# A graph network on one core: maximum pass and attention pass merged into one pass with a running maximum

## The chip, the core and the metric

The kernel runs on one NeuronCore of one Trainium2 chip. The time is that of one execution on the device in microseconds (us); lower is better. The engines have names here: PE is TensorE (its weight loads are PEld), DVE is VectorE, ACT is ScalarE, POOL is GpSimd, and SP is SyncE, which only issues DMAs in this kernel. DMA is a transfer between the chip's memories.

## The reference

12,500 nodes with 128 values each go through four layers, joined by 212,500 directed edges that are sorted by their end (`dst`) and go from `src` to `dst`. The change concerns the third layer, graph attention with 4 heads of 32 values. Its sums run over the edges of one `src` node (there the layer's `tgt` is `src`, and it gathers from `dst`):

```python
h = (node_features @ W + b).reshape(N, N_HEADS, F_HID)
s_i = jnp.einsum('nhf,hf->nh', h, a_i)
s_j = jnp.einsum('nhf,hf->nh', h, a_j)
eij = jax.nn.leaky_relu(s_i[tgt] + s_j[src], negative_slope=0.2)
m = jax.ops.segment_max(eij, tgt, num_segments=N)
ex = jnp.exp(eij - m[tgt])
denom = jax.ops.segment_sum(ex, tgt, num_segments=N)
alpha = ex / denom[tgt]
msg = alpha[:, :, None] * h[src]
out = jax.ops.segment_sum(msg, tgt, num_segments=N) + h
```

The other three layers (a relational convolution in two passes, a mean aggregation with batch norm, a plain mean aggregation) are not touched.

## The kernel before

The nodes lie in 98 blocks of 128. The edges are walked in steps: a step is up to 128 edges of one block, a group is K = 8 steps, and there are NG = 220 groups. Every edge pass runs the same way. POOL issues eight indirect DMAs for a group (`gather`, L1094), each of which brings 128 rows of `HROW` (128 values and 4 scores `s_j`, RW = 132 words) into a slot of the ring `G`, which has RING = 4 group slots. A one-hot matrix of 128 x 128 per step says which edge belongs to which node of its block, and PE multiplies with it.

The third layer has two edge passes.

`largest_pass` finds the largest `s_j` per node. Per group: POOL gathers the rows; SP stores them to `KEEP` in device memory (L1609); DVE splits the 32 scores per edge into three bf16 parts (`pieces`, L1735 to L1742, 5 instructions); PE turns them (5 transposes, L1655 and L1656) and ACT copies the result to `ROWS` (L1634). Then come four steps `pair(n)`: PE writes for two steps a matrix of 4 heads x 128 edges into two PSUM banks, where edges that are not of the node have a huge negative number (4 matmuls of 512 columns, L1665 and L1667, with the masks `MSEL` and `SEL` of the digits of the edge's place); DVE reduces them by maximum (`reduce`, L1750) and folds the result into `MJ` (`largest`, L1758, two per pair, each waiting for the one ahead). PE also runs 4 matmuls of 512 columns per group whose result nothing reads (L1677).

`attention_pass` then reads the groups back from `KEEP` (L1814), so POOL gathers nothing there. Per group: DVE builds the one-hots in bf16 (L1836), ACT casts them to f32 (`plain`, L1889), PE turns them (L1934) and ACT copies the turned ones (`turned`, L1897). PE looks up `s_i` and the maximum of every edge's node (`scores`, L1923, 8 matmuls in bf16), DVE makes the exponent (`exponents`, L1846 to L1855, 5 instructions), ACT takes exp (L1904), POOL multiplies the rows by it (L1876), PE clears three banks (`clear`, L1056) and sums with the one-hots (`main`, L1059, 8 f32 matmuls, which the trace shows as 16 records), and DVE adds the window of 9 blocks to `ACC` (`add_window`, L1066). Two windows of PSUM alternate.

On each engine the order is written by hand in `body(j, r)`, with offsets to groups further ahead. Block numbers come from tables in SBUF: `words_of` (L456) loads words into registers of the engine's queue, and behind it all instructions of that queue wait.

Of the kernel before, what the change touches and what calls it, by code (L numbers as in the profile page):

```python
# [9 lines left out]
P = 128  # L10
# [61 lines left out]
def build_gnn(nc, x, src, dst, etype, W1, loop1, b1, W2, loop2, b2, lw, lb, gamma, beta, gw, gb, attn, out):  # L72
# [5 lines left out]
    with ctx:  # L78
# [6 lines left out]
        POSA = sb("POSA", [P, SW])  # L85
# [39 lines left out]
        KEEP = dram("KEEP", [NG, P, K * RW])  # L125
# [338 lines left out]
        pool = [sem(f"work{i}") for i in range(20)]  # L464
# [1120 lines left out]
        READY = 35  # L1585
        MROW = 3 * K
        MBLOCKS = -(-NG * MROW // (2 * RW))

        def largest_pass(tag):
            fresh()  # L1590
            s_ids, s_pc, s_ts, s_sj, s_step, s_red, s_mx, s_c = (own(tag + n) for n in (
                "ids", "pc", "ts", "sj", "step", "red", "mx", "c"))
            s_got, s_st = [sem(tag + f"got{r}") for r in range(RING)], [own(tag + f"st{r}") for r in range(RING)]
            keep = KEEP.rearrange("g p w -> p g w")
            wtb, scrb = WT[:].bitcast(BF16), SCR[:].rearrange("p a c -> p (a c)").bitcast(BF16)
            SEL, MSEL = (wtb[:, i * K * P:(i + 1) * K * P].rearrange("p (k n) -> p k n", k=K) for i in range(2))
            ROWS = [scrb[:, i * 640:(i + 1) * 640] for i in range(2)]
            PLANES = [HT[:, i, :].bitcast(BF16)[:, HEADS * MROW:(HEADS + 1) * MROW] for i in range(2)]
            MPW = words.bitcast(BF16)[:, 0:NG * MROW]
            MP = MPW.rearrange("p (g m k) -> p g m k", m=3, k=K)  # L1600
            PIECES = [HT[:, i, :].bitcast(BF16)[:, 0:HEADS * 3 * K].rearrange("p (h q k) -> p h q k", h=HEADS, q=3) for i in range(2)]
            REST = SM[:, 1, :].rearrange("p (h k) -> p h k", h=HEADS)
            ROWST = PS[5].bitcast(BF16)[0:3 * K, 0:640]
            with nc.Block() as block:
                @block.sync
                def _(q):
                    def body(j, r, g):
                        q.wait_ge(s_got[r], 16 * K * (j + 1))
                        q.dma_start(keep[:, bass.ds(g, 1), :], G[:, r, :, :].rearrange("p k w -> p (k w)").unsqueeze(1)).then_inc(s_st[r], 16)  # L1609
                    groups(q, body)  # L1610
                    for s in s_st:
                        q.wait_ge(s, 16 * (NG // RING))
# [12 lines left out]
                def _(q):  # L1625
                    def ids(r, g):
# [513 lines left out]
```

## Time and profile before

| | |
|---|---|
| time, median of 3 runs | 13222.71 us (13216.57 to 13241.61) |
| the profiled execution's own time | 13216.57 us |
| its span in the trace | 13216.6 us |
| maximum pass, first piece to last reduction | 7817.3 to 10006.0 us |
| attention pass, first weights to end | 10021.2 to 10963.1 us |
| mean granted PE clock | 0.724 |

The profiled execution is one of the three timed ones, and its span is its time. Times inside the trace count from the span's start. A busy share says how long an engine worked, not that others waited for it; for that one needs the waits and the order in time.

### The profile page before, as it was taken

The page shows a single profiled execution, that of the slowest core. Times are in us where ns is not written, and L with a number is a line of the kernel's source. Part 1 is how long each engine was busy: PE and PEld are TensorE (multiplying, and loading weights), DVE is VectorE, ACT ScalarE, POOL GpSimd, SP SyncE. Part 2 cuts the span into 40 slices and gives each one's busy share as a digit, 9 for nine tenths or more (in the row PEclk, how much of TensorE's full clock was granted, in tenths as well). Part 3 has the DMA queues.
Part 4 walks back from the last instruction along what each step waited for, and adds up shares of the span by engine and source line. Part 5 has one row for each costly group of instructions (what it writes and reads, how often), then busy time and mean ns, then how long its engine had stood idle before and what let it go on. Part 6 is the DMA issues. An engine that isn't in the chain of part 4 may idle for free. (4 is left out here: it accounts for less than half of the span.)

```text
span 13216.6 us, 180443 instructions
## 1 busy us (share of the span) xinstructions
PE 7201.1 (54%) x38837; PEld 5498.7 (42%) x38948; DVE 7238.0 (55%) x15486; ACT 1724.0 (13%) x3850; POOL 8694.4 (66%) x9117
## 2 busy tenths in 40 slices
PE   7555655743333344444447956666668993333333
PEld 4444544433333344444446722222226772333333
DVE  5788888543333342222227976666667885333334
ACT  5000000200000022222220020000003552000000
POOL 0777777367777757777772137777775554777776
PEclk9777676866555566666668978888889996555665
DMA  5222222422222221111116823333333333222222
GB/s 189 63 52 52 52 52 52 152 73 53 53 53 53 53 56 53 53 53 53 53 53 168 202 85 108 108 108 108 108 109 116 126 126 83 54 54 54 54 54 66
DMA packets 704316, 1079.20 MB, mean 82 GB/s; under 512 B 174594, under 2 KB 483723, under 8 KB 704228
## 3 DMA queue, kind: packets, MB, share of 16 engines
q0 software_dynamic: 270832, 566.96, 16.8%
q1 hardware_dynamic: 301480, 449.08, 10.3%
q10 hardware_dynamic: 131916, 62.14, 1.8%
q8 instruction: 36, 0.59, 0.0%
q14 instruction: 52, 0.43, 0.0%
HBM read 717.19 MB, written 362.85 MB: 82 GB/s over the span
## 5 line engine op out<-in xcount | busy, mean ns | idle before, releaser
L1094 POOL DMA_INDIRECT G<-HROW,IDS x3424 | 3236.9, 945 | 1361.8 <-issue 1039.0
L1094 POOL DMA_INDIRECT G<-TAB,IDS x3328 | 3176.5, 954 | 1327.7 <-issue 996.6
L1194 PE MATMUL PSUM<-G,OH 128*128 x7040 | 1603.9, 420 | 2715.0 <-SPq L1126 2643.4
L1194 PEld LDWEIGHTS PSUM<-G,OH 128*128 128x128 f32 x7040 | 1491.9, 322 | 2827.0 <-issue 2827.0
L1433 POOL DMA_INDIRECT MSG<-G,IDS x1664 | 1617.0, 972 | 608.0 <-issue 506.5
L1421 PE MATMUL PSUM<-ACC,SCR 128*128 x3520 | 802.7, 417 | 974.9 <-ACT PSUM L1346 974.7
L1750 DVE TENSOR_REDUCE SM<-PSUM 128x8 f32<-128x1024 f32 x880 | 1077.2, 1224 | 398.4 <-PE PSUM L1667 301.1
L1177 DVE TENSOR_TENSOR ACC<-ACC,PSUM 128x129 f32 x1760 | 512.0, 291 | 1316.6 <-PE PSUM L1194 1090.6
L1177 DVE TENSOR_TENSOR X<-X,PSUM 128x128 f32 x1760 | 504.4, 287 | 1304.5 <-PE PSUM L1194 1076.0
L1421 PEld LDWEIGHTS PSUM<-ACC,SCR 128*128 128x128 f32 x3520 | 744.7, 317 | 1015.3 <-issue 1015.3
L1328 PE MATMUL PSUM<-G,OH 128*128 x3520 | 837.2, 414 | 588.0 <-DVE ACC L1090 390.3
L1394 DVE CAST SCR<-PSUM 128x1024 f32<-128x1024 bf16 x220 | 269.2, 1224 | 1541.9 <-PE PSUM L1410 1541.9
L1328 PEld LDWEIGHTS PSUM<-G,OH 128*128 128x128 f32 x3520 | 737.9, 310 | 626.5 <-issue 623.7
L1111 ACT COPY IDS<-IDXA 128x8 int32 (+1 forms) x624 | 122.3, 197 | 6087.4 <-PE PSUM L1194 4029.9
L1059 PE MATMUL PSUM<-G,OH 128*128 128x129 f32 (+1 forms) x7040 | 883.2, 279 | 29.2 <-DVE OH L1038 27.3
L1059 PEld LDWEIGHTS PSUM<-G,OH 128*128 128x128 f32 x7040 | 838.0, 191 | 112.4 <-issue 95.7
L1038 DVE TENSOR_TENSOR OH<-PSUM,DLOA 128x1024 f32<-128x1024 f32 x660 | 805.6, 1221 | 44.4 <-issue 42.8
L1876 POOL TENSOR_TENSOR G<-G 128x1024 f32<-128x1024 f32 x220 | 554.6, 2521 | 414.4 <-ACT G L1904 414.4
L1665 PE MATMUL PSUM<-SCR,WT 128*128 128x512 bf16 x1760 | 805.1, 457 | 36.8 <-DVE SM L1750 28.5
L1667 PE MATMUL PSUM<-SCR,WT 128*128 128x512 bf16 x1650 | 761.5, 462 | 0.0
L1066 DVE TENSOR_TENSOR ACC<-ACC,PSUM 128x1188 f32 x440 | 610.6, 1388 | 87.5 <-PE PSUM L1059 87.4
L1090 DVE TENSOR_TENSOR ACC<-ACC,PSUM 128x128 f32 x1760 | 500.2, 284 | 245.6 <-PE PSUM L1328 52.7
(348 smaller groups left out, 9577.3 us busy)
## 6 DMA issues: line engine op xcount, KB each, us to landing
KEEP<-G SPq DMA_DIRECT2D x220, 528.0 KB
G<-KEEP SPq DMA_DIRECT2D x220, 528.0 KB, 3.5
G<-MSG ACTq DMA_DIRECT2D x880, 66.0 KB, 2.2
G<-MSG SPq DMA_DIRECT2D x880, 66.0 KB, 2.1
G<-HROW,IDS POOLq DMA_INDIRECT x3424
G<-TAB,IDS POOLq DMA_INDIRECT x3328
TAB<-SCR SPq DMA_DIRECT2D x100, 512.0 KB, 2.6
TAB<-OH SPq DMA_DIRECT2D x96, 512.0 KB, 2.6
```

The lines of the kernel that those rows point to most:

```text
L1038: return q.tensor_tensor(OH[:, r % 2], bcast(iota.unsqueeze(1), P, K, P), bcast(dlo[:, bass.ds(g * K, K)].unsqueeze(2), P, K, P), op)
L1059: return q.matmul(window(n)[:, bass.ds(off, w)], hot, rows, start=False, stop=False, skip_group_check=True)
L1066: q.tensor_tensor(a, a, window(n).rearrange("p (a c) -> p a c", a=3)[:, :, 0:3 * RW], ALU.add).then_inc(s_add, 1)
L1094: q.indirect_dma_start(G[:, r, k, 0:row], None, table, bass.IndirectOffsetOnAxis(ap=IDS[:, r, k:k + 1], axis=0)).then_inc(s_got[r], 16)
L1177: q.tensor_tensor(a, a, sums(r, k), ALU.add).then_inc(s_add, 1)
L1194: m = q.matmul(sums(r, k), OH[:, r % 2, k, :], rows[k], start=True, stop=True)
L1328: m = q.matmul(slot(k)[:, 0:w], OH[:, r % 2, k, :], rows[k], start=True, stop=True)
L1421: m = q.matmul(PSUM[:, bass.ds(places[k], RW)], TURN[r % 2][:, k * P:(k + 1) * P], acc_of(regs[k], RW), start=False, stop=False, skip_grou ...
L1433: q.indirect_dma_start(MSG, bass.IndirectOffsetOnAxis(ap=IDS[:, r, k:k + 1], axis=0), G[:, r, k, :], None).then_inc(s_sc[r], 16)
L1665: q.matmul(bank.rearrange("p (h e) -> p h e", h=HEADS), MSEL[:, k, :], bcast(ROWS[r % 2][:, HEADS * P:(HEADS + 1) * P].unsqueeze(1), P, HE ...
L1667: m = q.matmul(bank, SEL[:, k, :], ROWS[r % 2][:, 0:HEADS * P], start=False, stop=True)
L1750: q.tensor_reduce(reduced(n), PSUM[:, (n % 2) * 1024:(n % 2 + 1) * 1024].rearrange("p (h e) -> p h e", e=P), AX.X, ALU.max).then_inc(s_red, 1)
```

## The change

`largest_pass`, `KEEP`, its stores and its reads are gone. One `attention_pass` gathers a group with POOL and keeps its rows in the ring `G` until they are summed. It holds a maximum per node that grows from group to group. After a group's maxima are folded in, `tops` writes the new exponent offsets of the 9 blocks of the group's window to `SI`, and keeps by how much the offset of the group's first block moved (`OLD`); ACT takes exp of that (`fade`), and DVE multiplies this block's sums in `ACC` by it (`rescale`). The one-hots no longer come from a comparison: PE multiplies the digit masks `MSEL` with `ROWS`, and ACT turns the result into 0 and 1 with a Relu with a bias (`plain`, `turned`). `scores` runs in f32 with 8 columns. The rows are weighted half by DVE (`weigh`, 4 steps) and half by ACT (`weights`, 16 instructions on 128 x 32). There is one window of sums (`SUMS`) where there were two. The 4 matmuls that nothing reads are gone. The order on each engine, with the group that each call works on relative to the body's group g:

- DVE: load of 8 block numbers; reduce 0 (g+1); rescale (g); exponents (g); reduce 1, largest 0 (g+1); weigh (g); reduce 2, largest 1 (g+1); pieces (g+2); reduce 3, largest 2 and 3 (g+1); tops (g+1); add (g)
- PE: scores (g); pair 1, 2, 3 (g+1); plain (g+1); rows (g+2); main (g); turned (g+1); pair 0 (g+2)
- ACT: ids (g+4); weights (g); plain (g+1); rows (g+2); turned (g+1); fade (g+1)
- POOL: the 8 gathers of one group after the other, each group after the ring slot's `main`

The diff, cut to its core:

```diff
-        KEEP = dram("KEEP", [NG, P, K * RW])
...
-        def largest_pass(tag):
...
+        def attention_pass(tag):
...
+            BANKS = [PSUM[:, i * 1024:(i + 1) * 1024] for i in range(2)]
+            SUMS = PSUM[:, 2048:3584]
+            ROWST = PS[7].bitcast(BF16)[0:3 * K, 0:640]
+            SCORES = PS[7][:, 320:320 + 2 * HEADS * K].rearrange("p (k h) -> p k h", k=K)
...
                 @block.gpsimd
...
                     def body(j, r, g):
                         q.wait_ge(s_ids, g + 1)
-                        wait(q, s_st[r], 16 * j)
-                        wait(q, s_pc, 5 * (g - RING + 1))
+                        wait(q, s_mm, g - RING + 1)
...
                         gather(q, r, HROW, RW, s_got)
...
+                    def weights(j, r, d):
...
+                        q.wait_ge(s_z, 4 * x + 4)
+                        q.activation(G[:, rx, :, D:RW], Z[rx % 2], ACT.Exp).then_inc(s_ex, 1)
+                        q.wait_ge(s_ex, x + 1)
+                        for k in range(K // 2, K):
+                            for h in range(HEADS):
+                                part_ = G[:, rx, k, h * HD:(h + 1) * HD]
+                                m = q.activation(part_, part_, ACT.Copy, scale=G[:, rx, k, D + h:D + h + 1])
+                        m.then_inc(s_wa, 1)
...
+                    def plain(j, r, d):
...
+                        q.wait_ge(s_hm, x + 1)
+                        wait(q, s_mm, x - 1)
+                        q.activation(OH[:, rx % 2].rearrange("p k n -> p (k n)"), BANKS[0], ACT.Relu, bias=ONES[:, 0:1], scale=1.0 / FAROFF).then_inc(s_of, 1)
...
+                    q.copy(ACC[:], bcast(ZERO[:, 0:RW].unsqueeze(1), P, NB, RW)).then_inc(s_clean, 1)
...
                 @block.tensor
...
+                    def scores(j, r, d):
...
+                        regs = blocks(q, BREGB, x)
+                        q.wait_ge(s_ot, x + 1)
+                        q.wait_ge(s_md, 4 * x + 4)
+                        wait(q, s_z, 4 * (x - 1) + 3)
+                        if there(x + 1):
+                            q.wait_ge(s_sj, x + 2)
+                        for k in range(K):
+                            m = q.matmul(SCORES[:, k, :], TURN[:, k, :], SIW[:, bass.ds(regs[k] * (2 * HEADS), 2 * HEADS)], start=True, stop=True)
...
+                    def plain(j, r, d):
...
+                        q.wait_ge(s_red, PAIRS * x + 3)
+                        for k in range(K):
+                            m = q.matmul(BANKS[0][:, k * P:(k + 1) * P], ROWS[rx % 2][:, HEADS * P:(HEADS + 1) * P], MSEL[:, k, :], start=True, stop=True)
...
+                    def main(j, r, d):
...
+                        places = words_of(q, REGS[96:97, :], x * 2 * K, K, 1536 - RW, first=K)
+                        wait(q, s_add, x)
...
                 @block.vector
...
+                    def weigh(j, r, d):
...
+                        q.wait_ge(s_ex, x + 1)
+                        rows = G[:, rx, own_part, 0:D].rearrange("p k (h f) -> p k h f", h=HEADS)
+                        q.tensor_tensor(rows, rows, bcast(G[:, rx, own_part, D:RW].unsqueeze(3), P, K // 2, HEADS, HD), ALU.mult).then_inc(s_wd, 1)
...
+                    def tops(j, r, d, first):
...
+                        [base] = words_of(q, GB, x, 1, NB - WIN, first=K)
+                        q.wait_ge(s_mx, (x + 1) * K)
...
+                        q.tensor_copy(OLD, was).then_inc(s_md, 1)
+                        q.tensor_tensor(TOPS, seen[:, :, 0:HEADS], MJW[:, bass.ds(base * HEADS, WIN * HEADS)].rearrange("p (b h) -> p b h", b=WIN),
+                                        ALU.add).then_inc(s_md, 1)
...
+                        q.scalar_tensor_tensor(seen[:, :, HEADS:2 * HEADS], TOPS, SLOPE, TOPS, ALU.mult, ALU.max).then_inc(s_md, 1)
...
+                        q.tensor_tensor(OLD, OLD, was, ALU.subtract).then_inc(s_md, 1)
...
+                    def rescale(j, r, d):
...
+                        [first] = words_of(q, BREGB, x * K, 1, NB - 1, first=K + 1)
+                        q.wait_ge(s_fe, x + 1)
+                        wait(q, s_add, x)
...
+                        q.tensor_tensor(rows, rows, bcast(FADE.unsqueeze(2), P, HEADS, HD), ALU.mult).then_inc(s_rs, 1)
+                        q.tensor_tensor(a[:, D:RW], a[:, D:RW], FADE, ALU.mult).then_inc(s_rs, 1)
...
+                        x, rx, jx = behind(j, r, 1)
+                        regs = blocks(q, BREGB, x) if there(x) else [None] * K
+                        reduce(j, r, 1, 0)
+                        rescale(j, r, 0)
+                        exponents(j, r, 0)
+                        reduce(j, r, 1, 1)
+                        largest(j, r, 1, 0, regs)
+                        weigh(j, r, 0)
+                        reduce(j, r, 1, 2)
+                        largest(j, r, 1, 1, regs)
+                        pieces(j, r, 2)
+                        reduce(j, r, 1, 3)
+                        largest(j, r, 1, 2, regs)
+                        largest(j, r, 1, 3, regs)
+                        tops(j, r, 1, regs[0])
+                        add(j, r, 0)
...
-        largest_pass("lp")
         attention_pass("at")
```

## Rows read from the trace of the kernel before

**Rows 1.** The page, part 1: busy time and share of the span of each engine.
```profile
PE 7201.1 (54%) x38837; PEld 5498.7 (42%) x38948; DVE 7238.0 (55%) x15486; ACT 1724.0 (13%) x3850; POOL 8694.4 (66%) x9117
```

**Rows 2.** Windows over the maximum pass and the attention pass: length, busy times, PE clock.
```profile
7817.30:10006.00 2188.70, 1387.06 (x5390) 543.70 (x5500) 1490.79 (x3737) 171.18 (x436) 1641.62 (x1741) 0.84 0.37 108
...
10021.20:10963.10 941.90, 860.47 (x7666) 739.55 (x7664) 802.68 (x1532) 480.43 (x657) 554.61 (x220) 1.00 0.38 124
```

**Rows 3.** Groups by line, maximum pass, 8200 to 9500 us: busy us, mean ns, idle before.
```profile
L1094 POOL DMA_INDIRECT G<-HROW,IDS x1042 | 983.1, 943 | 317.6 <-issue 317.6
L1750 DVE TENSOR_REDUCE SM<-PSUM 128x8 f32<-128x1024 f32 x520 | 636.6, 1224 | 234.8 <-PE PSUM L1667 180.8 <-issue 47.1
...
L1758 DVE TENSOR_TENSOR MJ<-MJ,SM 128x4 f32 x1041 | 166.5, 160 | 97.1 <-DVE MJ L1758 9.5
...
L1634 ACT COPY SCR<-PSUM 24x640 bf16<-24x640 bf16 x130 | 88.6, 681 | 1197.2 <-PE PSUM L1656 1197.2
```

**Rows 4.** Timeline, one group of the maximum pass: start us, us, instructions.
```profile
8409.73 1.06 DVE L1758 TENSOR_TENSOR MJ<-MJ,SM 128x4 f32 x4
...
8412.23 1.23 DVE L1750 TENSOR_REDUCE SM<-PSUM 128x8 f32<-128x1024 f32 x1 [1.43 <-issue]
...
8413.37 0.16 DVE L1735 COPY HT<-ACC 128x24 bf16 x1
...
8414.30 1.23 DVE L1750 TENSOR_REDUCE SM<-PSUM 128x8 f32<-128x1024 f32 x1
...
8414.36 0.60 PE L1655 MATMUL PSUM<-IDENTB,HT 128*24 128x128 bf16 x4 [3.45 <-DVE HT L1742]
...
8417.98 1.03 PE L1677 MATMUL PSUM<-USTB,LINB 128*128 128x512 bf16 x4
```

**Rows 5.** Line 456, maximum pass: the queue's load of 8 words, min/median/max ns.
```profile
L456 DVEq TENSOR_LOAD <-REGS x131: 594/597/612, 8200.2 to 9499.3; - x131
```

**Rows 6.** Windows inside one group of the maximum pass, columns as Rows 2.
```profile
8400.93:8404.35 3.42, 0.07 (x1) 0.07 (x2) 2.18 (x7) 0.00 (x0) 2.50 (x4) 0.93 0.34 89
8404.35:8407.76 3.41, 3.41 (x13) 1.44 (x14) 2.22 (x4) 0.78 (x2) 2.77 (x3) 0.57 0.56 188
```

**Rows 7.** Timeline, one group of the attention pass.
```profile
10406.54 0.61 PE L1934 MATMUL PSUM<-IDENTB,WT 128*128 128x128 bf16 x8
...
10406.98 0.67 PE L1056 MATMUL PSUM<-ZERO 128*128 128x396 bf16 x3
10407.09 0.19 DVE L1849 TENSOR_TENSOR SM<-SM,G 128x32 f32<-128x32 f32 x1
10407.18 1.01 ACT L1897 COPY SCR<-PSUM 128x1024 bf16<-128x1024 bf16 x1 [0.85 <-PE PSUM L1934]
...
10407.32 0.19 DVE L1851 SCALAR_TENSOR_TENSOR SM<-SM 128x32 f32<-128x32 f32 x1
10407.49 1.96 PE L1059 MATMUL PSUM<-G,OH 128*128 128x132 f32 x16
...
10409.59 1.39 DVE L1066 TENSOR_TENSOR ACC<-ACC,PSUM 128x1188 f32 x1 [0.39 <-PE PSUM L1059]
```

**Rows 8.** Line 456, attention pass: loads of 16 words and of 1 word.
```profile
L456 PEldq TENSOR_LOAD <-REGS x163: 1102/1104/1118, 10202.2 to 10896.4; - x163
L456 DVEq TENSOR_LOAD <-GB x163: 299/304/317, 10202.4 to 10896.7; - x163
```

**Rows 9.** Timeline, start of the maximum pass: gather beside DVE, DVE's clearing.
```profile
7802.53 1.99 DVE L1697 TENSOR_TENSOR ACC<-ACC 128x1760 f32<-128x1760 bf16 x1
7802.92 2.42 POOL L1094 DMA_INDIRECT G<-HROW,IDS  x1 [0.30 <-issue]
...
7808.76 8.64 DVE L1725 MEMSET ACC<- 128x10296 f32 x1 [2.21 <-issue]
```

**Rows 10.** Timeline, ACT: instructions with pointer operands, and the clearing of sums.
```profile
7773.27 1.65 ACT L658 ACTIVATE SCR<-X,NMR,RSTD 128x128 f32<-128x128 f32 x4
...
10008.39 2.39 ACT L1881 CAST ACC<-ZERO 128x2640 f32<-128x2640 bf16 x1 [13.42 <-PEq L475]
```

More of the change, by code:

```diff
@@ L461, in blocks @@
             return words_of(q, breg, g * K, K, NB - 1)
-        pool = [sem(f"work{i}") for i in range(20)]
+        pool = [sem(f"work{i}") for i in range(26)]
         assert [s.num for s in pool] == list(range(pool[0].num, pool[0].num + len(pool)))
@@ L1604, in largest_pass @@
-            with nc.Block() as block:
[L1605 to L1612, printed above, removed]
+            Z = [SM[:, 2 + i, :].rearrange("p (k h) -> p k h", k=K) for i in range(2)]
@@ L1614, in _, with behind, schedule, ring @@
+            def behind(j, r, d):
+                return j * RING + r + d, (r + d) % RING, j + (r + d) // RING
+            def schedule(q, early, body):
+                for i in range(-early, 0):
+                    body(0, i)
+                def ring(j):
+                    for r in range(RING):
+                        body(j, r)
+                rings(q, ring)
+            with nc.Block() as block:
                 @block.gpsimd
@@ L1640, in _, with ids @@
-                    for g in range(RING):
+                    def ids(x, rx):
+                        q.copy(IDS[:, rx, :], IDXB[:, bass.ds(x * K, K)]).then_inc(s_ids, 1)
+                    def weights(j, r, d):
+                        x, rx, jx = behind(j, r, d)
+                        if not there(x):
+                            return
+                        q.wait_ge(s_z, 4 * x + 4)
[6 more added lines that the diff above has]
+                        m.then_inc(s_wa, 1)
@@ new lines, in turned, with fade @@
+                    def turned(j, r, d):
+                        x, rx, jx = behind(j, r, d)
+                        if not there(x):
+                            return
+                        q.wait_ge(s_tm, x + 1)
+                        wait(q, s_sc, x)
+                        q.activation(TURN.rearrange("p k e -> p (k e)"), BANKS[1], ACT.Relu, bias=ONES[:, 0:1], scale=1.0 / FAROFF).then_inc(s_ot, 1)
+                    def fade(j, r, d):
+                        x, rx, jx = behind(j, r, d)
+                        if not there(x):
+                            return
+                        q.wait_ge(s_md, 4 * x + 4)
+                        wait(q, s_rs, 2 * x)
+                        q.activation(FADE, OLD, ACT.Exp).then_inc(s_fe, 1)
@@ L1641, in _, with body @@
+                    def body(j, r):
+                        x, rx, jx = behind(j, r, 4)
+                        if there(x):
+                            ids(x, rx)
+                        weights(j, r, 0)
+                        plain(j, r, 1)
+                        rows(j, r, 2)
+                        turned(j, r, 1)
+                        fade(j, r, 1)
+                    for g in range(2):
                         ids(g, g)
-                    rows(0, 0)
-                    ringed(q, body)
+                    q.wait_ge(s_c, READY)
@@ L1681, in _, with body @@
+                    def body(j, r):
+                        scores(j, r, 0)
+                        for n in range(1, PAIRS):
+                            pair(j, r, 1, n)
+                        plain(j, r, 1)
+                        rows(j, r, 2)
+                        main(j, r, 0)
+                        turned(j, r, 1)
+                        pair(j, r, 2, 0)
+                    schedule(q, 2, body)
                 @block.vector
@@ L1961, in build_gnn @@
+                    schedule(q, 2, body)
         tables_and_first("d0", load_relations(W1, loop1, b1))
```

364 lines of the change are left out of this document (136 added, 228 removed).

## The prediction

> **What bounds the kernel now.** I read the page first: no engine is busy for more than 66% of the span, so each pass has its own limit [rows 1]. Then the windows of the two passes that the change touches, then the lines, the timeline and the queue's loads of each.
>
> The maximum pass runs from 7817.3 to 10006.0, so 2188.7 / 220 = 9.95 us a group [rows 2]. The lines say why: a gather takes 943 ns and POOL's queue needs another 317.6 / 1042 = 305 ns before the next, so eight take 9.98 us, the whole group [rows 3]. POOL waits for nobody there; DVE (68% busy) and PE fit under it.
>
> The attention pass takes 941.9 / 220 = 4.28 us a group, with PE 91% busy at the full 2.4 GHz [rows 2]. There PE is the bound; DVE adds the window 0.39 us after PE let it [rows 7].
>
> Together a group costs 14.23 us, and both passes with the seam between them last from 7817.3 to 10963.1.
>
> **The change, part by part.** The 8 gathers stay, but POOL has only them: 9.98 us a group is the floor. Storing to and reading from `KEEP` goes, and is worth nothing by itself: neither pass waits for it. The seam goes too (15.2 us). Everything else of both passes now has to fit into one body, and the body's period T decides. So I add up DVE, from start to start, and then walk the waits.
>
> DVE, per group:
> - 4 reductions: one starts 1.14 us ahead of what follows it (8412.23 to 8413.37) [rows 4]: 4.56 us.
> - `largest`: four in a chain take 1.06 us, so 0.30 us each and 0.16 for the last [rows 4]. Pairs 0 and 1: 0.30 + 0.20 each, 1.00; pairs 2 and 3: three gaps, 0.90.
> - `pieces`: 8413.37 to 8414.30, 0.93 us [rows 4].
> - `exponents`: now 4 instructions on 128 x 32, one every 0.23 us [rows 7]: 0.92 us.
> - `rescale`: 128 and 4 columns. Not in the trace; between 0.16 for 4 columns [rows 3] and 0.19 for 32 [rows 7] for each, plus 0.1 for the wider: 0.40 us. Its load hides under reduction 0.
> - `weigh`: 512 columns, both inputs in SBUF. 1760 such columns take 1.99 us [rows 9] and 32 take 0.19 [rows 7], so 1.04 ns a column and 0.69 us; 0.61 from start to start. Bounds: 0.53 without any fixed part, and 1.55 if it has to wait for a whole gather (0.94 [rows 3]) each time; the small instructions with two SBUF inputs beside the gathers show no such wait (0.16 for 4 columns), so I stay low.
> - `tops`: nothing long lies ahead of it to hide its load of one word, 0.30 us [rows 8]. DVE's queue needed 1.43 us ahead of reduction 0 before, of which 0.60 is the load of 8 words [rows 4, 5]; the rest, 0.83, is unpacking, waits, addresses and a loop branch. For `tops` I take 0.30 + 0.60 of those, then four small instructions with computed addresses at 0.25: 1.66 us until its last starts.
> - `add`: again a bare load, 0.30 + 0.45 of queue steps, then 1.39 us [rows 7, 8], 1.30 from start to start; the load of 8 block numbers for the next body (0.60) hides under it, but for a branch every fourth time (0.1 on average): 2.15 us.
>
> Sum: 4.56 + 1.00 + 0.90 + 0.93 + 0.92 + 0.40 + 0.61 + 1.66 + 2.15 = 13.1 us. DVE alone would give T = 13.1, so what POOL and PE cost one after the other before (14.23) would be cheaper by 1.1 us a group.
>
> ACT, per group: ids 0.2, exp 0.25, 16 scalings, two Relus at 1.05, rows 0.68, fade 0.25. A scaling is not in the trace. Four instructions with two pointer operands on 128 columns take 1.65 us with 0.48 for the last alone, 0.39 apart [rows 10]; 96 columns fewer at 0.83 ns (0.68 and 1.01 us for 640 and 1024 columns bound that slope [rows 3, 7]) leaves 0.31. The floor is 0.19. I take 0.31: 5.0 us, 8.5 in all, under 13.1. Of one such instruction, the Trainium skill (ScalarE: Activation LUTs, What ACT_TABLE_LOAD costs) gives 186 ns + 0.83 ns a column + 93 ns for a pointer, with 93 ns of overlap. By that a scaling costs 0.21 us, and the sum of ACT falls to 6.9; T is the same by both.
>
> PE at full clock: `scores` and `main` are 16 records each, 1.96 us; 12 + 4 matmuls of 512 columns at 1.03 - 0.17 = 0.86 per pair, 3.4 us; plain and turned 0.5 each, rows 0.6, clears 0.5 [rows 4, 7]. That is 9.3 us of a body.
>
> **The walk.** Zero is the start of reduction 0. DVE: exponents (g) at 1.54, reduction 1 at 2.5, reduction 2 at 4.7, pieces (g+2) from 6.35 to 7.3, reduction 3 at 7.3, tops done at 11.1, add (g) at 11.7, next reduction 0 at 13.1. PE can turn the rows of g+2 only at 7.3. Behind them in its queue stands the load of 8 places for `main`: 1.10 us for 16 words [rows 8], 0.60 for 8 [rows 5]. After the transposes' dispatch (0.5) come load and unpacking (0.9), so clears start at 8.7 and `main` at 9.2, ending at 11.1. The scalings ended at 2.5 + 0.3 + 5.0 = 7.8 and are not late; `add` at 11.7 is not held either. Then `turned` on PE to 11.7, its Relu on ACT to 12.8, the waits and addresses of `scores` 0.2, `scores` to 15.0. DVE wants it at 13.1 + 1.54 = 14.6. It is 0.4 late: T = 13.5 at the full clock, and now the loop pieces, rows, main, turned, scores, exponents is the bound, with DVE just under it. The bound has moved to waits.
>
> The order in this loop is what makes the clock count. Before, PE sat idle for 3.45 us in each group [rows 4], and the stretch behind that was granted 0.57 of the clock, nearly all of it at the lower level of 1.2 GHz [rows 6]; it cost nothing, because POOL was the bound. In the new body PE has only pair 3 and plain (1.3 us) between the end of pair 2 (about 3.2) and the rows at 7.3, each after a reduction. The four idle matmuls that filled in before are gone. So I expect a like stretch at 1.2 GHz once a body, 3.4 us long as in rows 6, and just where rows, clears and `main` run, which are 2.9 us of the loop. At half speed such a stretch does 1.7 us of work less; the queue's load absorbs 0.3 of it. T = 13.5 + 1.4 = 14.9.
>
> **The sum.** Start: DVE's preparation ends at 7808.8, where it cleared part of `ACC` before [rows 9]; ACT clears all 12,936 columns instead. 2640 took 2.39 us [rows 10], so 11.7 us, and the first pieces start at about 7820 where they started at 7817.3. 220 bodies and two that run ahead with half their work are 221 T. The end is at 7820 + 221 x 14.9 = 11113, against 10963 before: +150 us. The profiled execution's time is 13216.6, all of it span, and becomes 13367; the median lies 6.1 higher: 13373, say 13370. In general the time is 10080 + 221 T, and no change lies at T = 14.22. A change within 0.2% (26 us) can hardly be told from none.
>
> **The rivals.**
> 1. DVE stays the bound, as PE's short gaps do not take the clock down. For it: pairs and plain break the idle time up, and PE works 9.3 of 13.5 us. Against it: in the maximum pass a nearly empty window was followed by one at 0.57 [rows 6], and here 1.3 us in 4.1 is not much more. T = 13.4 to 13.6, time 13060. It decides from T = 14.1 down. Chance 0.28.
> 2. Two stretches at half clock in a body, or one that never ends: rows, main, turned and scores are 6 us of work; another 1.8 us lost gives T = 16.7, time 13770. Against it: PE at half clock is busy for most of the body, which brought the clock back within one window before. Chance 0.10.
> 3. The gathers become the bound again. Beside instructions of DVE on 1760 columns a gather took 2.42 us, not 0.94 [rows 9]; beside `pieces` and `largest` they did not stretch [rows 3]. `weigh` meets one or two gathers a group, for 10.7 to 11.5 us in all, under T. It would need four at 2.4: 16 us, time 13616. Chance 0.03. By the Trainium skill (SBUF — State Buffer, Who interferes with whom), DVE and GpSimd share a port pair, an instruction of DVE with two SBUF inputs contends with GpSimd instructions that read SBUF, and the loser waits for the whole instruction. By that rule `weigh`, `rescale` and `tops` speak against this change, since either side may be the one that waits.
> 4. The ring starves: a gather may start only after `main` of four groups ago. It then has from 11.1 to 2T + 6.35 = 36, and needs 10 us and a few to land. Chance 0.02.
> 5. The change is only a trade: T lands within 0.12 of 14.22. Chance 0.08.
>
> **How the numbers follow.** The forecast, slower with T between 14.4 and 15.9 (13262 to 13594 by itself), has 0.49. With rivals 2 to 4 slower has 0.64, same 0.08, faster 0.28. The range has to hold rival 1 but for its fastest end, T = 13.4 (13040), and reaches to T = 16.4 (13700) above: 0.8 together.
>
> **What the profile after would show.** The stretch as one pass of about 3290 us; POOL idle before gathers, waiting for `main` of four groups ago; a DVE wait before exponents for `scores`, 0.4 us if the clock is full and 1.5 to 2 if not; PE's clock at 0.8 to 0.9 in the pass; ACT waiting for `turned`. The walk is wrong if DVE waits ahead of a reduction or of `pieces`; the sum is wrong if DVE's queue needs more than 0.9 us ahead of `tops` or `add`; the clock step is wrong if the pass shows 1.00 or under 0.7.

## The result, and the profile after

The changed kernel takes 13301.22 us (median of 4, 13288.21 to 13321.94) beside 13220.29 us for the kernel before (median of 4, 13216.57 to 13241.61). The ratio is 1.006, with a 95% interval of 1.0046 to 1.0074: slower by 0.6%, 81 us. Forecast were 13370, the range 13040 to 13700, and slower with a chance of 0.64. The profiled execution is the slowest of the four (13321.94 us, span 13320.1); the rest of this section is read from it.

Part 1 of the page, beside [rows 1]. No engine is near full; ACT has gained most, by the scalings.
```profile
PE 7349.2 (55%) x41367; PEld 5824.4 (44%) x41588; DVE 7216.4 (54%) x16580; ACT 2582.6 (19%) x7590; POOL 8163.6 (61%) x8897
```

The new pass as one window, first reduction to last `add`, columns as [rows 2]:
```profile
7835.50:11062.60 3227.10, 2398.69 (x15612) 1609.09 (x15829) 2284.55 (x6375) 1502.70 (x4836) 1648.81 (x1741) 0.89 0.16 37
```
The adds start from 7856.85 to 11062.59 in 219 steps, so the period between two adds is T = 14.64 us, where 14.9 was forecast and 14.22 would have been no change. DVE is busy for 71% of the pass, PE for 74%, POOL for 51%. Nobody is full: the pass is held by waits. The clock is 0.89.

The groups by line, 9000 to 10500 us (102 groups; columns as [rows 3]):
```profile
L1094 POOL DMA_INDIRECT G<-HROW,IDS x813 | 769.9, 947 | 727.8 <-PE PSUM L1781 390.6 <-issue 337.2
L1865 DVE TENSOR_REDUCE SM<-PSUM 128x8 f32<-128x1024 f32 x407 | 497.2, 1222 | 79.5 <-issue 68.6 <-PE PSUM L1736 9.2
...
L1781 PE MATMUL PSUM<-G,OH 128*128 128x132 f32 x1616 | 268.7, 336 | 0.0
...
L1943 DVE TENSOR_TENSOR ACC<-ACC,PSUM 128x1188 f32 x101 | 140.6, 1392 | 131.2 <-PE PSUM L1781 123.3 <-issue 7.9
...
L1901 DVE TENSOR_TENSOR G<-G 128x512 f32<-128x512 f32 x102 | 70.5, 691 | 0.0
...
L1887 DVE TENSOR_TENSOR SM<-PSUM,G 128x32 f32<-128x32 f32 x101 | 19.2, 190 | 40.2 <-PE PSUM L1717 40.2
```
A gather takes 947 ns beside `weigh`, as it did without it, and `weigh` never waits. POOL stands before gathers until `main` (L1781) has freed the ring. PE's transposes (L1765) wait for `pieces` in each group, 85.3 us in 102 times, and `scores` waits for the Relu behind `turned` 94 times (48.1 us): the loop of the prediction's walk is there. DVE waits in two places of each group: 123.3 / 101 = 1.22 us ahead of `add` for `main`, and 40.2 / 101 = 0.40 ahead of the exponents for `scores` (L1717). And there is a line that the prediction had nothing for: reductions (L1865) wait 68.6 us for "issue".

From the list of waits, same stretch: us in total, times, longest.
```profile
DVE ACC L1943 <- PE PSUM L1781: 123.3, 85, 2.5
...
PE PSUM L1765 <- DVE HT L1857: 85.3, 102, 1.1
...
DVE SM L1865 <- issue: 68.6, 24, 3.1
```
The last line is 24 waits of 2.86 us, not 400 small ones. The stretch holds 26 turns of the loop. The timeline shows which reduction it is, DVE alone:
```profile
9305.97 1.39 DVE L1943 TENSOR_TENSOR ACC<-ACC,PSUM 128x1188 f32 x1 [1.27 <-PE PSUM L1781]
9310.24 1.23 DVE L1865 TENSOR_REDUCE SM<-PSUM 128x8 f32<-128x1024 f32 x1 [2.88 <-issue]
...
9322.74 1.39 DVE L1943 TENSOR_TENSOR ACC<-ACC,PSUM 128x1188 f32 x1 [1.65 <-PE PSUM L1781]
...
9336.30 1.39 DVE L1943 TENSOR_TENSOR ACC<-ACC,PSUM 128x1188 f32 x1 [0.49 <-issue]
```
It is reduction 0, behind the fourth `add` of a ring, where DVE's queue jumps back to the start of its loop. The queue's own records of line 1070 (the loop's end), 9000 to 10500: times, shortest/median/longest ns, first and last start.
```profile
L1070 DVEq COMPARE_BRANCH  x26: 62/63/63, 9008.9 to 10487.0; - x26
...
L1070 DVEq FUSED_REGOPS  x26: 105/105/105, 9011.7 to 10489.8; - x26
```
The branch starts at 9008.9 and takes 0.06; the next instruction starts at 9011.7. Over all the turns of the pass the gap, from the end of the branch to the next instruction, has a median of 2.76 us. In the maximum pass of the kernel before it was 0.23. It shows in the periods between adds, by their place in the ring: 13.76, 13.98, 14.26 and 16.75 us (means from the 20th group on).

Five packets of the instruction queue go with each turn, and the page counts 314 of them, beside 52 for the kernel before:
```profile
q14 instruction: 314, 2.57, 0.1%
```

Now the clock, in windows over one slow body (the `add` of 9305.97 to that of 9322.74) and one fast (to 9336.30):
```profile
9313.60:9317.00 3.40, 2.92 (x12) 1.20 (x12) 2.89 (x11) 2.71 (x13) 2.02 (x3) 0.50 0.21 48
9317.00:9320.40 3.40, 2.41 (x12) 1.79 (x13) 2.33 (x9) 1.80 (x2) 0.00 (x0) 0.50 0.06 14
...
9327.20:9330.60 3.40, 1.81 (x9) 0.47 (x7) 3.21 (x6) 3.37 (x17) 2.63 (x3) 1.00 0.25 60
9330.60:9334.00 3.40, 1.83 (x19) 1.34 (x20) 2.71 (x11) 2.06 (x4) 1.89 (x2) 1.00 0.24 60
```
and PE in both bodies:
```profile
9318.69 1.17 PE L1776 MATMUL PSUM<-ZERO 128*128 128x396 bf16 x3 [0.48 <-issue]
9319.66 2.82 PE L1781 MATMUL PSUM<-G,OH 128*128 128x132 f32 x16
...
9333.17 0.67 PE L1776 MATMUL PSUM<-ZERO 128*128 128x396 bf16 x3 [0.75 <-issue]
9333.68 1.96 PE L1781 MATMUL PSUM<-G,OH 128*128 128x132 f32 x16
```
At 1.2 GHz clears and `main` are slow and `add` waits 1.65 us; at 2.4 GHz `main` takes 1.96 and `add` starts after 0.49 us of DVE's own queue. The fast body lasts 13.56 us. Of 1500 us, 370 were granted half the clock, 3.6 us a group. They are not spread evenly: by place in the ring a body has 1.2, 2.9, 2.6 and 7.3 us of it (means from the 20th group on), and the 7.3 are in the body with the jump, where PE waits for the late reduction 0 as well (0.90 us at 9311.52, and the pairs behind it are slow). So the jump and the clock are not independent of each other.

### The profile page after: what moved, and what is told of

It reads as the page before. It is cut to its first block and busy times, and to the rows that moved or that the text cites. A ratio compares the mean times of both kernels' runs of the same rounds, so it can differ in the third digit from the quotient of the medians.

```text
span 13320.1 us, 189431 instructions
## 1 busy us (share of the span) xinstructions
PE 7349.2 (55%) x41367; PEld 5824.4 (44%) x41588; DVE 7216.4 (54%) x16580; ACT 2582.6 (19%) x7590; POOL 8163.6 (61%) x8897
## 5 line engine op out<-in xcount | busy, mean ns | idle before, releaser
L1194 PEld LDWEIGHTS PSUM<-G,OH 128*128 128x128 f32 x7040 | 1496.0, 323 | 2828.2 <-issue 2828.2
L1865 DVE TENSOR_REDUCE SM<-PSUM 128x8 f32<-128x1024 f32 x880 | 1075.1, 1222 | 165.8 <-issue 135.4
L1328 PEld LDWEIGHTS PSUM<-G,OH 128*128 128x128 f32 x3520 | 739.3, 310 | 631.8 <-issue 629.1
L1734 PE MATMUL PSUM<-SCR,WT 128*128 128x512 bf16 x1760 | 715.9, 407 | 164.4 <-DVE SM L1865 150.6
L1651 ACT ACTIVATE G<-G 128x32 f32<-128x32 f32 x3520 | 771.8, 309 | 7.1
L1736 PE MATMUL PSUM<-SCR,WT 128*128 128x512 bf16 x1540 | 625.3, 406 | 0.0
L1781 PEld LDWEIGHTS PSUM<-G,OH 128*128 128x128 f32 x3520 | 578.1, 246 | 32.2 <-issue 24.8
L1781 PE MATMUL PSUM<-G,OH 128*128 128x132 f32 x3520 | 567.4, 329 | 4.2 <-ACT G L1651 4.2
L1717 PEld LDWEIGHTS PSUM<-SI,SCR 128*128 128x128 f32 x3520 | 410.4, 192 | 216.2 <-issue 216.2
```

Of the source, the lines that this page charges most:

```text
L1194: m = q.matmul(sums(r, k), OH[:, r % 2, k, :], rows[k], start=True, stop=True)
L1328: m = q.matmul(slot(k)[:, 0:w], OH[:, r % 2, k, :], rows[k], start=True, stop=True)
L1651: m = q.activation(part_, part_, ACT.Copy, scale=G[:, rx, k, D + h:D + h + 1])
L1734: q.matmul(bank.rearrange("p (h e) -> p h e", h=HEADS), MSEL[:, k, :], bcast(rows_[:, HEADS * P:(HEADS + 1) * P].unsqueeze(1), P, HEADS, P ...
L1736: m = q.matmul(bank, SEL[:, k, :], rows_[:, 0:HEADS * P], start=False, stop=True)
L1781: m = q.matmul(SUMS[:, bass.ds(places[k], RW)], OH[:, rx % 2, k, :], G[:, rx, k, :], start=False, stop=False, skip_group_check=True)
```

## The experiments

So there were two candidates for what a body costs above 13.5: the jump back of DVE's loop (theory A, that DVE waits for instructions) and PE's half clock (the clock step of the prediction, B). A third question was what the loads in the queues cost. All ratios are against the kernel before, on the same chip. The three sets of runs were on three chips, where the kernel before takes 13237.97, 13216.56 and 13220.16 us, so runs of different sets are compared by ratios and by T.

**Padding that was none.** Two kernels with empty instructions ahead of DVE's loop:
```
                     assert c.n == READY, c.n
+                    for _ in range(96):          # second kernel: 256
+                        q.nop(nofuse=True)
                     q.wait_ge(s_clean, 1)
```


> The changed kernel with 96 empty instructions on DVE just ahead of the loop of the new pass, run once; nothing else differs. Theory A (instruction fetch): DVE's loop of four bodies has 322 instructions and lies over the border of what its instruction store holds, so every jump back waits 2.75 us for instructions. 96 instructions further on it lies within two lines of 256. Then the gap after DVE's loop branch falls from 2.75 us to 0.2, the long fourth period (16.8 us) becomes like the other three (13.6 to 14.2), the packets of the instruction queue fall from 314 to under 100, and the time falls by up to 54 x 2.75 = 148 us, to 13150 to 13190: faster than the kernel before. Theory B (the fourth body is long because of what its instructions wait for, scores and a clock at half speed, and the jump back only shows it): the gap and the periods stay, 13300.

> As the run with 96, but with 256 empty instructions, one whole line of 256, so that the loop lies as it did against the lines. Theory A: nothing changes; the gap of 2.75 us stays, every fourth period is 16.8 us, 13300 (13290 to 13320). If empty instructions help in some other way than by where the loop lies, the time falls as with 96.

13294.02 us, ratio 1.004 (1.0026 to 1.0054), and 13296.04 us, 1.0044 (1.0027 to 1.0061); gaps of 2.73 us and 314 packets in both. But the compiled program is one instruction longer than that of the changed kernel in both cases, so these empty instructions moved nothing. The two runs test neither theory. They are worth keeping as repeats: T is 14.61 and 14.51, beside 14.64. Differences of T of 0.1 are no more than that spread. Of the figure in the first text: the Trainium skill (Runtime: NRT & Kernel Launch, Instruction fetch mechanics) says that the store is two lines of 256 instructions and that a jump to an instruction outside them waits for a fetch.

**The clock.**
```
+                    def busy(n):
+                        for _ in range(n):
+                            q.matmul(PSUM[:, 3468:3580], LINB[:], USTB[:, 0:112], start=True, stop=True, ...)
...
                         for n in range(1, PAIRS):
                             pair(j, r, 1, n)
+                            busy(12 if n > 1 ... else 0)
                         plain(j, r, 1)
+                        busy(12 ...)
```


> The changed kernel with 36 more matmuls a body on PE, whose result nobody reads (112 columns each, into columns of PSUM that nothing uses): 12 behind pair 2, 12 behind pair 3, 12 behind plain; DVE's code stays where it was. The clock step of my prediction: PE's idle time there brings a stretch at 1.2 GHz in each body, on the path rows, clears, main, turned, scores; with the clock at 2.4 GHz throughout, a body loses 0.7 us and more: 13301 - 221 x 0.7 = 13146, and 12990 if it was 1.4. Rival (DVE is the bound in three bodies of four, and the jump in the fourth): the clock goes up from 0.87 to 0.95 and more, the wait of exponents for scores goes, and the time falls by its 0.40 us a group at most, to 13210 to 13300.

13165.16 us, ratio 0.9945 (0.9928 to 0.9961), T = 13.92: now the kernel is faster than before the change. The gap at the jump is unchanged, 2.73. Groups by line, 9000 to 10500:
```profile
L1781 PE MATMUL PSUM<-G,OH 128*128 128x132 f32 x1712 | 210.1, 276 | 0.0
...
L1949 DVE TENSOR_TENSOR ACC<-ACC,PSUM 128x1188 f32 x107 | 149.0, 1392 | 55.1 <-PE PSUM L1781 41.7 <-issue 13.4
```
`main` costs 210.1 / 107 = 1.96 us a group where it cost 268.7 / 101 = 2.66, and the wait of `add` for it falls from 1.22 to 0.39. T fell by 0.72, about these 0.70. The half clock has become less and has moved: 218 us of 1500 are still at 1.2 GHz, no record of `main` is stretched any more, and what is stretched are a quarter of the pairs and a seventh of the added matmuls. The three short periods are 13.55, 13.19 and 13.51.

**The loads.** DVE's two loads of a window base and PE's load of eight places, moved ahead (with the 96 empty instructions, which do nothing):
```
+                        y = behind(j, r, 0)[0]
+                        top = words_of(q, GB, x, 1, NB - WIN, first=K)[0] if there(x) else None
+                        base = words_of(q, GB, y, 1, NB - WIN, first=K + 2)[0] if there(y) else None
                         reduce(j, r, 1, 3)
...
-                        tops(j, r, 1, regs[0])
-                        add(j, r, 0)
+                        tops(j, r, 1, regs[0], top)
+                        add(j, r, 0, base)
...
+                        places = places_at(j, r, 0)
                         rows(j, r, 2)
-                        main(j, r, 0)
+                        main(j, r, 0, places)
```


> The kernel with 96 empty instructions, and three loads of registers moved ahead of waits: DVE's window base for tops and for add ahead of reduction 3, PE's eight places for main ahead of the transposes. If DVE's queue ahead of tops and add is on the path (my sum had 0.30 us for each bare load), the time falls against the run with 96 by up to 221 x 0.6 = 130 us, to 13020 to 13060. If the loop rows, main, turned, scores, exponents is the bound and only PE's load counts, it falls by 221 x 0.3 = 65 us or less, and DVE waits longer for scores or for main. If DVE's queue had these loads done while the engine worked, nothing changes.

13122.85 us, ratio 0.991 (0.9893 to 0.9926), T = 13.72. It took off more than both loads of DVE together could (0.9 of T against 0.6), so PE's load counts too, and `main` is slow less often (303 ns a record for 336). The waits say more:
```profile
DVE SM L1871 <- issue: 174.3, 137, 3.2
...
DVE ACC L1947 <- PE PSUM L1784: 20.8, 31, 1.3
```
DVE's loads are hardly hidden in their new place: besides the jump, reduction 3 (L1871) now stands 0.84 us for issue in each body, where `tops` and `add` had 0.60 and 0.49. What has gone is the wait of `add` for `main`, 1.22 us a group before and 0.19 now. That points to PE's load as the source of the gain; but the three were moved together, and no run parts them.

**Where DVE's loop lies.** Real instructions instead of empty ones, in the time in which DVE waits for ACT's clearing:
```
                     assert c.n == READY, c.n
+                    spare_columns = SM[:].rearrange("p a c -> p (a c)")
+                    for i in range(119):         # others: 16, 55
+                        c.inc(q.memset(spare_columns[:, i:i + 1], 0.0))
+                    c.hold()
                     q.wait_ge(s_clean, 1)
```


> The empty instructions of the first two runs never reached the program: it grew by one instruction, DVE's loop stayed where it was, and so they tested nothing. Here 119 real ones stand in their place, each a memset of one column that nobody reads, during 13 us in which DVE waits for ACT's clearing anyway. In the compiled program DVE's loop of 322 instructions then begins at instruction 3423, not at 3304. Theory A (fetching instructions): where the loop lies decides whether the jump back waits. The gap after DVE's loop branch falls from 2.75 to about 0.2 us, every fourth period comes down from 16.7 us to 14.0, packets of the instruction queue fall from 314 to under 100, and the time falls by up to 54 x 2.75 = 148 us, to about 13150, faster than the kernel before. Theory B (the fourth body is long for other reasons): gap, periods and time stay. By the Trainium skill (Runtime: NRT & Kernel Launch, Instruction fetch mechanics) the store holds two lines of 256 instructions; in the changed kernel the loop touches three such lines if they are counted from the start of DVE's program (it starts at place 232 of one), here two (it starts at place 95).

> The same with 16 memsets for 119: the loop begins at instruction 3320. Theory A: nothing changes against the changed kernel, gap 2.75 us, 13290 to 13320. If memsets ahead of the loop help in another way than by its place, the time falls here too. By the skill's page named with the run of 119, the loop (place 248) still touches three lines.

119 memsets: 13285.68 us, ratio 1.0053 (1.0036 to 1.007), gap 2.76, 315 packets, T = 14.51. 16 memsets: 13296.09 us, 1.0059 (1.0042 to 1.0076), gap 2.81, 315 packets, T = 14.62. The first expectation of A failed: by lines of 256 the loop should have fitted. With 119 memsets and the moved loads as well, and with the matmuls on top:

> 119 memsets and the loads of registers moved ahead. Without the memsets the moved loads gave 13123, T = 13.72 and a gap of 2.93 us. Theory A: T falls by up to 0.70 to 13.0, the time to 12970 to 13000. If the three other bodies of a ring are held by DVE's own sum (12.8 to 13.3 us between adds there), the fourth comes to the same 12.8 to 13.3 and no lower.

> All three: memsets, moved loads, and the 36 more matmuls a body that keep PE's clock up. Theory: clock and loads each took something off the same three bodies (13.35, 13.03, 13.31 with the clock; 12.83, 12.76, 13.30 with the loads; 13.6 to 14.0 with neither). If PE's part of the loop and DVE's queue are two parts of one chain, both gains add: T about 12.5, 12870. If DVE's own sum is the floor (12.5 with both loads hidden, my 13.1 less 0.6) the clock gives little more: T 12.7 to 13.0, 12900 to 12980.

13112.84 us, 0.992 (0.9904 to 0.9937), T = 13.81, and 13090.95 us, 0.9906 (0.9889 to 0.9922), T = 13.66. The gap stayed in both, 2.81 and 2.94 us. The matmuls give only 0.15 on top of the loads (22 us, more than either kernel's runs scatter), where they gave 0.72 alone: with the loads moved, the wait of `add` for `main`, which they took away, was down to 0.19 already.

The times at which packets of the instruction queue start, set against DVE's queue, corrected the theory:

> 119 memsets moved DVE's loop by 119 instructions, and the gap at the jump stayed. But the transfers of the instruction queue moved with it. In all runs there are five packets of 8192 bytes in a turn of the loop: two right behind the jump back (1.0 and 3.7 us after it), and three later, which start when DVE's queue stands at instruction 27, 155 and 283 of the loop in the changed kernel (loop from instruction 3304), 35, 164, 292 with 119 memsets (from 3423) and 11, 138, 266 with 16 (from 3320): each time two or three past a multiple of 128. So instructions come in pieces of 128 (8192 bytes), the next one is fetched when the queue enters a piece, and in all these places the loop lies in four pieces. Theory A2: four pieces and the one fetched ahead don't fit, so the jump back finds its own piece gone; three pieces and one do fit. 55 memsets put the loop at 3359 to 3680, in three pieces. Then the gap falls from 2.75 to 0.2 us, packets fall from 315 to about 60, the fourth period of a ring comes down to 14.0, and the time is 13130 to 13170, faster than the kernel before. Rival A3: a loop of over 256 instructions never stays, wherever it lies: nothing changes, 13290.

The places of the queue in this text are read 1.0 us ahead of the start of each packet, which is the time from the jump to the start of its first packet.

13254.03 us, ratio 1.0025 (1.0014 to 1.0036). The queue's records of line 1070 and the instruction queue, with 55 memsets:
```profile
L1070 DVEq COMPARE_BRANCH  x26: 56/56/56, 9036.6 to 10484.5; - x26
...
L1070 DVEq FUSED_REGOPS  x26: 105/105/105, 9036.9 to 10484.8; - x26
```
```profile
q14 instruction: 56, 0.45, 0.0%
```
The gap is 0.24 us, and the packets in the loop are gone, all of them. Sixteen, 55 and 119 memsets differ in nothing but where the loop of 322 instructions lies. In four pieces of 128 it is fetched anew in each turn; in three it stays. All the runs shown here agree: the nine programs with the loop in four pieces have the gap and five packets a turn, the three with 55 memsets have neither. A3 (too long, wherever it lies) has fallen, and so have two lines of 256, wherever one lets them start: no start gives two lines to the loop from 3359 and three to those from 3304, 3320 and 3423. But the time did not do what was expected: T is 14.37, not 13.95. The five programs with the body unchanged and the gap have 14.51 to 14.64, so removing the gap gave 0.14 to 0.27, 0.2 in the mean, of the 0.63 that it takes. The periods are 14.89, 14.01, 13.71 and 15.12. The fourth lost 1.6 us and the first gained 1.1. The lists by line and of waits say what took the place of the gap. `main` is nearly as slow as it was (326 ns a record) and `add` still waits 1.03 us a group for it; the exponents (L1891) wait 0.60 for `scores`, for 0.40, since in the fourth body the gap had hidden that wait; and reductions (L1869) wait 0.26 for pairs, for 0.09:
```profile
L1781 PE MATMUL PSUM<-G,OH 128*128 128x132 f32 x1664 | 264.9, 326 | 0.0
L1947 DVE TENSOR_TENSOR ACC<-ACC,PSUM 128x1188 f32 x104 | 144.8, 1392 | 117.4 <-PE PSUM L1781 107.5 <-issue 9.9
```
```profile
DVE SM L1891 <- PE PSUM L1717: 61.7, 103, 0.9
...
DVE SM L1869 <- PE PSUM L1736: 26.9, 36, 0.9
```

So the same 55 memsets should be worth more where the clock no longer holds the body:

> The run with 119 memsets, moved loads and more matmuls, with 55 memsets for 119; nothing else differs. It gave 13091 with T = 13.66, a gap of 2.94 us and periods of 12.65, 13.36, 12.97 and 15.67. A2: the fourth comes down to 12.7 to 13.3, T = 13.0, 12940 to 12960. A3: 13090.

12995.01 us, ratio 0.9828 (0.9812 to 0.9845), T = 13.21 with periods of 13.04, 13.15, 12.81 and 13.84, where 119 memsets had T = 13.66. Here the place of the loop is worth 0.45 of T, about 100 us by the ratios. The fourth period keeps 0.8 over the rest that the gap does not explain; DVE idles 0.3 us ahead of its reduction 0, which the other bodies don't, and the rest is not accounted for.

> The same with 55 memsets, but DVE's two loads of one word stand behind reduction 3 instead of ahead of it. Ahead of it they cost 0.83 us of DVE's time in each body in the trace with 119 memsets (the reduction's idle time before it, which nothing but its queue explains); behind it they lie under the 1.23 us of the reduction. If DVE's own sum is the bound, T falls by 0.8 against the other placing, to 12.2, and the time by up to 176 us, to 12780 to 12830 if A2 holds. If main or scores is what the three short bodies wait for, it falls by less than 0.4 a body, to 12860 to 12950.

12980.38 us, ratio 0.9818 (0.9802 to 0.9834), T = 13.18: almost nothing. What became of the 0.8 us is in the two lists of waits (L1879 are the reductions, L1901 the exponents, L1955 is `add`). Loads ahead of reduction 3:
```profile
DVE SM L1879 <- issue: 103.8, 142, 0.9
DVE SM L1901 <- PE PSUM L1717: 24.8, 48, 0.7
```
and behind it:
```profile
DVE SM L1901 <- PE PSUM L1717: 71.1, 114, 0.7
DVE ACC L1955 <- PE PSUM L1784: 42.4, 71, 0.9
...
DVE SM L1879 <- issue: 8.5, 28, 0.3
```
The wait of the reductions for issue went from 103.8 to 8.5 us, 0.84 a group, and waits of the exponents for `scores` and of `add` for `main` came in its place. DVE has slack now, and it is not the bound. What is, these two runs leave open. The loop of the walk is one candidate. The other is PE's own queue, which the 36 matmuls have filled. The last run, 9000 to 10500, columns as [rows 2], and two of its waits:
```profile
9000.00:10500.00 1500.00, 1379.79 (x12148) 1016.07 (x12263) 1189.48 (x3295) 772.63 (x2493) 861.64 (x908) 0.91 0.18 41
```
```profile
PE PSUM L1765 <- issue: 23.4, 66, 0.4
...
PE PSUM L1765 <- DVE HT L1871: 17.4, 48, 0.6
```
PE is busy for 92%, 1.05 us of a body of 13.2 are left to it, and the transposes wait for `pieces` in 48 groups of 114 only, where they did so in 102 of 102 in the changed kernel. In the other 66 they come behind PE's own work.

| kernel | ratio | T | periods by place in the ring | gap |
|---|---|---|---|---|
| changed | 1.006 | 14.64 | 13.76, 13.98, 14.26, 16.75 | 2.76 |
| 55 memsets | 1.0025 | 14.37 | 14.89, 14.01, 13.71, 15.12 | 0.24 |
| matmuls | 0.9945 | 13.92 | 13.55, 13.19, 13.51, 15.53 | 2.73 |
| loads | 0.991 | 13.72 | 12.97, 12.85, 13.37, 15.75 | 2.93 |
| 119, loads, matmuls | 0.9906 | 13.66 | 12.65, 13.36, 12.97, 15.67 | 2.94 |
| 55, loads, matmuls | 0.9828 | 13.21 | 13.04, 13.15, 12.81, 13.84 | 0.25 |
| same, DVE's loads later | 0.9818 | 13.18 | 12.89, 12.98, 13.19, 13.71 | 0.25 |

55 memsets with the matmuls and no load moved were not run. That would have shown T for the body as it was changed, with `main` at the full clock and without the gap. Nor were 55 memsets with the loads moved and no more matmuls, which would tell PE's own queue from the loop of the walk.

## Why the prediction was right, and where it was not

The number and the sign were right, and so was the body at the full clock, by the sum and by the walk. That the whole came so close was luck: the clock step was rated too high, and a cost of about the same size was missing.

- **Floor of the gathers, rivals 3 and 4**: right that they do not decide. A gather takes 947 ns (943 before), and POOL waits for `main` 3.8 us a group (390.6 / 102). Of the rule that rival 3 takes from the Trainium skill (SBUF — State Buffer, Who interferes with whom), this trace shows next to nothing: `weigh` has a mean of 691 ns over 102, with no idle time before it, and only a handful of gathers start well inside it. In the experiments, where the two meet otherwise, one side of the rule shows. In the run with the matmuls:
```profile
9561.09 0.69 DVE L1907 TENSOR_TENSOR G<-G 128x512 f32<-128x512 f32 x1
9561.15 1.45 POOL L1094 DMA_INDIRECT G<-HROW,IDS  x1 [0.31 <-issue]
```
  This gather started 0.63 us before `weigh` ended and took 1.45 us for 0.95; the 45 that start within a `weigh` in that run have a mean of 1.11. So the gather waits for `weigh`, as the rule has it. The other side does not show: a `weigh` that starts within a gather takes its 0.69. None of this costs time here, as POOL has slack.
- **DVE's sum, 13.1**: right within 0.2, but for the jump. The fast body takes 13.56 us, of which 0.67 is a wait for `scores`, so 12.9 of its own. `weigh` 0.69 as put in; the queue ahead of `tops` and of `add` leaves 0.60 and 0.49 us idle, less than the 0.9 that would have made the sum wrong.
- **ACT**: a scaling was put at 0.31; the trace has sixteen in 3.51 us, 0.22 each:
```profile
9312.80 3.51 ACT L1651 ACTIVATE G<-G 128x32 f32<-128x32 f32 x16
```
  ACT is busy for 1502.7 / 220 = 6.8 us a group. That is the 0.21 and the 6.9 that the prediction worked out from the Trainium skill (ScalarE: Activation LUTs, What ACT_TABLE_LOAD costs), and not my estimate from the rows. As it said, T is the same by both.
- **The walk, 13.5 at the full clock**: right. The fast body has 13.56, the mean of the three short periods with the matmuls is 13.42, and `scores` is late by 0.28 there (29.9 / 107; forecast 0.4). In the changed kernel the loop that the prediction named is the bound together with DVE: transposes wait for `pieces` in every group, exponents for `scores` in 75 of 101, and with the loads moved, of which PE's shows as 0.64 us of idle time ahead of the clears (65.7 / 102), most of the wait for `main` was gone. That the same loop is what holds T at 13.2 in the last two runs is not shown. By the prediction's own sign the walk was wrong in one place: DVE waits ahead of a reduction, at the jump.
- **The clock step, +1.4**: the mechanism is right, the size is a third to a half. The half clock comes as forecast, 3.6 us a group (3.4), the pass shows 0.89 (0.8 to 0.9), and filling PE's idle time gave back 0.72 of T. The wait that it makes stands elsewhere than forecast: 1.5 to 2 us ahead of the exponents were expected and 0.40 are there, while `add`, which the walk did not see held, waits 1.22 for `main`. The step put the stretch "just where rows, clears and `main` run" in every body. It falls there in some only: 0.39 of the records of `main` were stretched (over 1.3 times their 276 ns at the full clock), and `main` lost 0.70 us a group. Rival 1, full clock, had the body right and the clock wrong; rival 2 did not come.
- **The jump back, the step that failed**: the `add` term has "a branch every fourth time (0.1 on average)". The branch costs DVE's queue 2.76 us, 0.7 a group, since the body, four times over, is 322 instructions long, and where it lies it takes four pieces of 128. The loop of the maximum pass had 200 and a gap of 0.23. None of the rivals had this.
- **How the two add up**: 13.5 for the body, 0.5 for the clock (the three short periods have a mean of 14.0) and 0.7 for the jump make 14.7; 14.64 were measured. That is a way to book them, not a measurement of each: over half of the half clock falls into the body with the jump, and there the gap hides the wait for `scores`. Removed by itself, with the other present, the clock gave 0.72 and the jump 0.14 to 0.27, and the jump gave 0.45 with clock and loads out of the way. Forecast was 13.5 + 1.4. So 14.9 came close because one term was 0.7 or 0.9 too large and another 0.6 too small. The sign had luck in it too: with the measured clock loss and the 0.1 that the prediction had for the branch, the sum gives 14.1, below the 14.22 of no change. What the kernel did without the gap was milder, T = 14.37 and 0.25% slower, since other waits came up.
- **The start**: pieces were to begin at 7820 and began at 7831.0. ACT's clearing took 10.97 us (forecast 11.7) and begins when DVE's preparation ends, at 7819.9. That is 11 us later than before the change, though the preparation is as long as it was (21.5 us for 21.3): the untouched part ahead ran late in this execution, with the first `add` of the pass ahead at 7031.7 for 7018.5. In the experiments pieces begin between 7816.7 and 7836.0. The formula for the profiled execution has 10074 for 10080, and 10074 + 221 x 14.64 = 13309; 13321.9 were measured, and the late start is most of the difference.

What is open: why the fourth body is still 0.8 us longer without the gap, why 36 matmuls moved the half clock to the pairs and did not remove it, and what holds T at 13.2.

## What to carry to other kernels

Where two loops are merged, add up the instructions of one turn for each queue, and look in the trace for the gap behind each loop's branch: here the same 322 instructions cost 2.76 or 0.24 us a turn by where they lay, and 55 cheap instructions ahead of them decided it. A wait that shows in the trace is worth what stands behind it: removing the jump's 0.7 us a group gave 0.2 alone and 0.45 after two other waits had gone, so price it together with the next one in the chain. And where an engine idles between short steps on the path, the clock it gets is part of the price of its own instructions: 0.7 us of 14.6 here, bought back with 36 matmuls whose result nothing reads. They have a price as well: with them PE is busy for 92% of the last runs, and may itself be what holds them.

## What was not expected of the hardware

- DVE's instructions came in packets of 8192 bytes, 128 instructions each. Two of the five packets of a turn start 1.0 and some 3.7 us behind the jump. 1.0 us ahead of the start of each of the other three, the queue stood one to three instructions past a multiple of 128 of DVE's program, in three placings of the loop (from 3304, 3320 and 3423) and in nearly every turn; at their start it is 2 to 15 past. The Trainium skill (Runtime: NRT & Kernel Launch, Instruction fetch mechanics) has the mechanism, a jump out of what is held waits for a fetch, and the runs agree. They do not agree with its two lines of 256: by those, the loop from 3423 would have stayed, and it did not, and no other start of the lines fits all four placings. Four pieces of 128, of which one is fetched ahead, would fit all placings; that the store works so was not shown directly.
- PE's loop of 420 instructions, and of 564 with the matmuls, showed no gap at its branch (0.11 us at most).
- A gather that starts while `weigh` runs ends later by about what was left of `weigh`: 1.45 us for 0.95 in the run with the matmuls.
